# Softmax row sums of a 32-head attention: DMA chains that begin where ACT writes, all partial sums joined by DMA, one ones' product per head

## What is computed

```python
x = x + 0.5 * ffn(layernorm(x))             # weights are signs
x = x + attention(layernorm(x))
x = x + 0.5 * ffn(layernorm(x))

q, k, v = proj(w_q), proj(w_k), proj(w_v)   # 2 batches x 16 heads, head size 32
scores = jnp.einsum('bhqd,bhkd->bhqk', q, k) * SCALE
probs = jax.nn.softmax(scores, axis=-1)     # over 2048 keys
attn = jnp.einsum('bhqk,bhkd->bhqd', probs, v)
```

## Time and profile before

| | us |
|---|---|
| median of three runs (lowest, highest) | 2971.15 (2968.48, 2972.31) |
| profiled execution | 2973.73 |
| its span, first to last instruction | 2971.9 |
| PE busy | 2902.3 (98%) |
| DVE busy | 2038.9 (69%) |
| ACT busy | 1596.2 (54%) |
| POOL busy | 1382.4 (47%) |
| mean granted TensorE clock | 0.993 of full speed |

### The profile page before, as it was taken

The page is one execution under the profiler, slowest core; times in us unless marked ns, Lnnn a source line. Parts: engine busy times, 40 slices in busy tenths (PEclk is TensorE's granted clock), DMA queues, the critical chain, the costliest instruction groups (busy, mean ns, idle before and its releaser), DMA issues. The chain is left out here.

```text
span 2971.9 us, 38475 instructions
## 1 busy us (share of the span) xinstructions
PE 2902.3 (98%) x14528; PEld 1940.8 (65%) x14528; DVE 2038.9 (69%) x3036; ACT 1596.2 (54%) x2847; POOL 1382.4 (47%) x522
## 2 busy tenths in 40 slices
PE   7999998999999999999999999999999989999999
PEld 6888886887755555555555555555555458887887
DVE  5555555777788787878787888788888445555553
ACT  5444433332276666666666666666666644333333
POOL 0000000000089898988898988888888720000000
PEclk9999999999999999999999999999999999999999
DMA  4110112565398999898999898989898872222210
GB/s 184 30 56 29 29 34 79 185 197 169 123 224 199 226 202 231 200 234 198 228 204 229 202 232 201 228 203 231 203 228 208 212 209 57 57 57 57 57 29 29
DMA packets 189274, 459.97 MB, mean 155 GB/s; under 512 B 90272, under 2 KB 91296, under 8 KB 148768
## 3 DMA queue, kind: packets, MB, share of 16 engines
q0 software_dynamic: 36720, 267.40, 39.1%
q1 hardware_dynamic: 152368, 190.11, 22.4%
HBM read 121.91 MB, written 67.63 MB: 64 GB/s over the span
## 5 line engine op out<-in xcount | busy, mean ns | idle before, releaser
L918 DVE TENSOR_REDUCE att_row_max<-bank 128x1 f32<-128x512 f32 x2048 | 1255.3, 681 | 313.8 <-PE bank L989 313.7
L973 ACT ACTIVATE att_p<-bank 128x512 f32<-128x512 f32 x2048 | 1035.6, 629 | 411.9 <-PE bank L985 404.8
L874 POOL TENSOR_TENSOR att_acc<-att_acc,att_p 128x2048 f32<-128x2048 f32 x217 | 1063.4, 4901 | 34.3 <-ACT att_p L973 29.7
L985 PE MATMUL bank<-att_q,att_k 98*128 98x512 f32 x2048 | 849.6, 416 | 14.0 <-ACT att_p L973 9.2
L989 PE MATMUL bank<-att_k,att_q 96*128 96x512 f32 x2048 | 809.7, 397 | 11.0 <-DVE att_row_max L918 11.0
L985 PEld LDWEIGHTS bank<-att_q,att_k 98*128 98x128 f32 x2048 | 384.6, 188 | 391.4 <-issue 202.7
L1016 PE MATMUL bank<-att_p,att_v 128*32 128x512 f32 x4096 | 495.1, 600 | 0.0
L563 ACT ACTIVATE ffn_hid<-bank,up_s 128x512 f32<-128x512 f32 x256 | 176.1, 688 | 534.2 <-PE bank L591 519.8
L516 DVE TENSOR_TENSOR ffn_hid_lo<-ffn_hid,ffn_hid_hi 128x512 fp32r<-128x512 f32 x256 | 174.6, 687 | 376.5 <-ACT ffn_hid_hi L566 376.4
L989 PEld LDWEIGHTS bank<-att_k,att_q 96*128 96x128 f32 x2048 | 389.9, 190 | 61.7 <-DVE att_row_max L918 13.3
L591 PE MATMUL bank<-hi,ffn_up_w 128*128 128x512 f32 x1024 | 402.0, 393 | 3.8 <-DVE lo L189 3.8
(11 more groups left out here) (111 smaller groups left out, 2225.6 us busy)
## 6 DMA issues: line engine op xcount, KB each, us to landing
att_dma_acc<-att_p POOLq DMA_DIRECT2D x225, 1024.0 KB, 8.9
att_dma_acc<-att_dma_acc POOLq DMA_DIRECT2D x30, 1024.0 KB, 12.2
x<-x_after_ffn SPq DMA_DIRECT2D x16, 1024.0 KB, 7.5
att_q<-q_hi SPq DMA_DIRECT2D x64, 256.0 KB, 4.1
att_k<-k_hi SPq DMA_DIRECT2D x64, 256.0 KB, 10.1
x_after_ffn<-x_out SPq DMA_DIRECT2D x8, 1024.0 KB, 9.6
q_hi<-qkv_o_hi SPq DMA_DIRECT2D x32, 256.0 KB, 2.0
q_lo<-qkv_o_lo SPq DMA_DIRECT2D x32, 256.0 KB, 2.3
```

Source lines behind the costliest of these rows:

```text
L874: self.nc.gpsimd.tensor_tensor(self.acc[H % 2][:], a[:], self.prob[kt % PR][:], ALU.add).then_inc(self.summed, 1)
L918: self.nc.vector.tensor_reduce(self.row_max[odd][:, qt, q:q + 1], m[:], axis=AX.X, op=ALU.max).then_inc(self.m_read, 1)
L973: self.nc.scalar.activation(self.prob[kt % PR][:, q * CH:(q + 1) * CH], self.s_ps[(UNITS * H + kt * QC + q) % SR][:], ACT.Exp, scale=SCALE ...
L985: self.nc.tensor.matmul(self.s_ps[i % SR][:], self.k_st[H % NB][0:KM, kt * P:(kt + 1) * P], self.q_st[H % NB][0:KM, q * CH:(q + 1) * CH], ...
```

## The change

Three things change in how the denominators are made, and with them the places of four other steps.

1. `in_place(H, kt)` is true for the first tile of each chain (tiles 1 and 3). ACT writes these two directly into `dma_acc[H % 2][0]` and `[1]`, and PE's `out_tile` reads them there (`tile`). The two copying DMAs of a head are gone. The first adding DMA of each chain (tiles 5 and 7) now waits until PE has used that tile (`p_used`).
2. `join_sum` is a new adding DMA on POOL's queue, in the next head at tile 5: `acc` onto `dma_acc[..][0]`. It waits for POOL's last add, and for the landing of `join_chains`.
3. `sums` is one ones' product for heads 0 to 29 (`all_joined`) instead of two. It waits for the landing of `join_sum`, and stands after group 5 instead of 3. Heads 30 and 31 keep their three products.
4. Because the sums come later, ACT's `copy_sums` moves from tile 8 to tile 12 of the next head, SP sends `max_rows` before `move_sums`, and DVE's `invert` and SP's `store_inverse` come one head later (`invert` at tile 2).

The core of the diff:

```diff
-SUMS_AFTER = 3
+SUMS_AFTER = 5
 def sums_after(H):
-    return SUMS_AFTER if H < NH - 1 else SUMS_AFTER - 1
+    return SUMS_AFTER if H < NH - 1 else 2
-def chains_joined(H):
+def all_joined(H):
     return H < NH - 2
+def in_place(H, kt):
+    return kt in moved(H)[:CHAINS]
+    def tile(self, H, kt):
+        return self.dma_acc[H % 2][moved(H).index(kt)] if in_place(H, kt) else self.prob[kt % PR]
     def move(self, pool, H, kt):
+        if i // CHAINS == 1:
+            pool.wait_ge(self.p_used, KT * H + moved(H)[x] + 1)
-        if moved(H).index(kt) < CHAINS:
-            if H >= 2:
-                pool.wait_ge(self.t_ready, H - 1)
-            pool.sem_inc(self.move_begun, 1)
-            self.nc.gpsimd.dma_start(into[:], self.prob[kt % PR][:]).then_inc(self.dma_summed[x], 16)
+    def join_sum(self, pool, H):
+        pool.wait_ge(self.summed, all_adds(H))
+        pool.wait_ge(self.chains_joined, 16 * (H + 1))
+        if H > 0:
+            pool.wait_ge(self.sum_joined, 16 * H)
+        pool.sem_inc(self.move_begun, 1)
+        self.nc.gpsimd.dma_start(self.dma_acc[H % 2][0][:], self.acc[H % 2][:], accum_op=ALU.add).then_inc(self.sum_joined, 16)
-        if H > 0 and kt == (14 if H < NH - 1 else 12):
+        if H > 1 and kt == 2:
+            self.head_out.invert(dve, H - 2)
+        if H == NH - 1 and kt == 12:
             self.head_out.invert(dve, H - 1)
     def tile_free(self, act, H, kt):
+        if in_place(H, kt):
+            if H >= 2:
+                act.wait_ge(self.t_ready, H - 1)
+            return
     def sums(self, pe, H):
+        if all_joined(H):
+            pe.wait_ge(self.sum_joined, 16 * (H + 1))
+            self.ones_product(out, first, True, True).then_inc(self.t_ready, 1)
+            return
@@ SP, head H
                     if H > 0:
                         head_out.store_out(sp, H - 1)
+                    if H > 1:
+                        head_out.store_inverse(sp, H - 2)
+                    else:
+                        att.max_rows(sp, H + 1)
                     if H > 0:
                         head_out.move_sums(sp, H - 1)
-                    if H < LAST:
-                        att.max_rows(sp, H + 1)
@@ POOL, head H
                         if 0 < H < LAST and kt == 0:
                             att.join_chains(pool, H - 1)
+                        if 0 < H < LAST and kt == 5:
+                            att.join_sum(pool, H - 1)
```

More of the change, by code:

```diff
@@ L792, in moves_to @@
     i = moved(H).index(kt)
-    return sum(len(moved(h)[i % CHAINS::CHAINS]) for h in range(H)) + i // CHAINS + 1
+    return sum(len(moved(h)[i % CHAINS::CHAINS]) - 1 for h in range(H)) + i // CHAINS
 def all_adds(H):
@@ L903, in pool_tile @@
             self.add(pool, H, kt)
-        elif kt in moved(H):
+        elif kt in moved(H) and not in_place(H, kt):
             self.move(pool, H, kt)
@@ L967, in scalar_tile @@
         self.tile_free(act, H, kt)
+        into = self.tile(H, kt)
         if H > 0 and kt == G * (sums_after(H) + 1):
@@ L1015, in out_tile @@
             rows = slice(q * HD, (q + 1) * HD)
-            ins = self.nc.tensor.matmul(self.o_ps[rows, :], self.v_st[H % NB][:, kt, :], self.prob[kt % PR][:, q * CH:(q + 1) * CH],
+            ins = self.nc.tensor.matmul(self.o_ps[rows, :], self.v_st[H % NB][:, kt, :], self.tile(H, kt)[:, q * CH:(q + 1) * CH],
                                         start=(kt == 0), stop=(kt == KT - 1))
@@ L1027, in sums, with ones_product @@
     def sums(self, pe, H):
-        out, first, last = self.sums_bank(H), not direct(H), not chains_joined(H)
-        pe.wait_ge(self.summed, all_adds(H))
+        out, first = self.sums_bank(H), self.dma_acc[H % 2][0]
+        if all_joined(H):
+            pe.wait_ge(self.sum_joined, 16 * (H + 1))
+            self.ones_product(out, first, True, True).then_inc(self.t_ready, 1)
+            return
+        pe.wait_ge(self.summed, all_adds(H))
+        self.ones_product(out, self.acc[H % 2], not direct(H), False)
+        for x in range(CHAINS):
+            pe.wait_ge(self.dma_summed[x], 16 * all_moves(H, x))
+            ins = self.ones_product(out, self.dma_acc[H % 2][x], False, x == CHAINS - 1)
+        ins.then_inc(self.t_ready, 1)
+    def ones_product(self, out, tile, start, stop):
         for q in range(QC):
             rows = slice(q * HD, (q + 1) * HD)
-            self.nc.tensor.matmul(out[rows, :], self.ones_sum[:], self.acc[H % 2][:, q * CH:(q + 1) * CH], start=first, stop=False)
-        for x in range(CHAINS if last else 1):
-            if last:
-                pe.wait_ge(self.dma_summed[x], 16 * all_moves(H, x))
-            else:
-                pe.wait_ge(self.chains_joined, 16 * (H + 1))
-            for q in range(QC):
-                rows = slice(q * HD, (q + 1) * HD)
-                ins = self.nc.tensor.matmul(out[rows, :], self.ones_sum[:], self.dma_acc[H % 2][x][:, q * CH:(q + 1) * CH],
-                                            start=False, stop=(x == CHAINS - 1 or not last))
-        ins.then_inc(self.t_ready, 1)
+            ins = self.nc.tensor.matmul(out[rows, :], self.ones_sum[:], tile[:, q * CH:(q + 1) * CH], start=start, stop=stop)
+        return ins
     def bank_free(self, pe, H, at):
```

21 lines of the change are left out of this document (12 added, 9 removed).

## The result

Five runs beside five of the kernel before gave a median of 2955.86 us (2954.83 to 2960.73) against 2971.15 us (2968.48 to 2973.02): ratio 0.995, 95% interval 0.9937 to 0.9962. The change gains 15.3 us; the forecast was 2941, a gain of 30.2. The time lies just inside the upper edge of the range (2956), and the sum was twice too large.

The account below looks back on a forecast made before the run. PE's queue was taken to set the head. One ones' product fewer, head 31's end and head 1 summed to 25.8 + 4 + 1 = 30.8 us, from median 2971.15 to 2940.4, rounded to 2941; range 2934 to 2956.

Parts of the forecast that it names:

- What bounds the kernel: Ordinary heads: PE's queue, with work in 48.96 of 49.10 us, sets the head, with POOL close behind.
- rival A: POOL sets the head, which shortens by 3.7 us, 111 in 30 heads, giving 2860 us; chance 0.02.
- The product's price, 0.86: Heads 0 to 29: one ones' product fewer on PE saves 0.86 us each, 25.8 in all; its new place costs 0.
- rival B: Group 6 gets crowded or small waits return 12 to 20 us: 2950 to 2962 us; chance 0.14.
- The join of the accumulator: PE's new wait: the join lands at T = 29, 6 us before PE wants the sums; stall 0.
- Rival D: The accumulator's join lands after T = 35.4, PE waits 3.7 us a head: slower, 3056 us; chance 0.09.
- Tile 5's DMA: On POOL, behind the new wait: goes out at about T = 21.2 instead of 23.7; cost 0.
- SP's order: Maxima rows go no later; the sums behind them land 2.9 us before DVE wants them; cost 0, bounds 0 and 1 a head.
- So the queue carries 7 x 5.16 = 36.1 us a head after, 6 x 5.16 + 5.2 = 36.2 before: no more load: POOL's DMA queue with the copies gone: equal load, so no gain or cost in ordinary heads.
- Rival C: Next head's maxima rows come 0.9 us later in every head, so nothing is gained: about 2970 us; chance 0.06.
- The end of head 31: Without the two copies, POOL's load, scaling and last chain DMAs come earlier: gain 4 us, bounds 0 and 5.2.
- Head 1: POOL is late there from the extra split of output weights; an earlier POOL may give another 1 us, taken as 1.

Follow-up runs that it names:

- without_tile_9: Changed kernel without tile 9's adding DMA in heads 0 to 29, so it computes something else: 2939.00 us, ratio 0.9891.
- two_products: Changed kernel without the join of POOL's accumulator; PE makes two ones' products a head, after group 5: 2962.59 us, ratio 0.9967.
- turn_earlier_spread: Changed kernel, POOL's second feed-forward sign weights after DVE's, maxima six tiles ahead instead of four, early ones two a step at most: 2946.24 us.
- in_place_alone: Kernel before with only tiles 1 and 3 written in place by ACT and the two copies gone: 2964.33 us, ratio 0.9977.
- tile_13_behind_add: Changed kernel, POOL's second feed-forward sign weights after DVE's, tile 13's DMA issued behind POOL's add of tile 14: 3019.36 us.
- sums_sent_later: Changed kernel with SP's transfers of the sums, the reciprocal and its store one head later: 3062.14 us, ratio 1.0312.
- pool_after_dve: Changed kernel with POOL making its piece of the second feed-forward's sign weights only after DVE has made its own: 2949.99 us, ratio 0.9924.
- low_row_from_act: Changed kernel, POOL's second feed-forward sign weights after DVE's, second maxima row issued by ACT in tile 14 instead of SP: 2945.16 us.

## Why the prediction was right and wrong, step by step

- **What bounds the kernel: right.** Taking a product off PE's queue shortened the head wherever the rows were in time (48.02). The rule of the Trainium skill named in the prediction (Perfetto Trace Analysis, Identifying the Most-Contended Engine) would have made POOL the bound: the trace does not agree, POOL has as much work as before (1372.8 us, 1382.4 before), and the head followed PE (rival A).
- **The product's price, 0.86: right**, and its new place at no cost too (5.01 us for group 6, where over 4.3 + 0.86 would have been rival B). without_tile_9 gave 1.03 a head (49.05 - 48.02), two_products, which keeps both products, 0.11.
- **The join of the accumulator: right.** It was to land at T = 29 after 8.2 us; it landed at 27.2 after 7.9, and PE waited for it nowhere. Rival D, at 3056 the costly one, did not come.
- **Tile 5's DMA: right** (T = 21.2 forecast, 19.9 measured). **SP's order: right** as far as PE and DVE go: DVE does not wait for `head_tot_t`.
- **"So the queue carries 7 x 5.16 = 36.1 us a head after, 6 x 5.16 + 5.2 = 36.2 before: no more load", "No gain or cost in ordinary heads": the step that failed.** It put the price of the new order of POOL's transfers at nothing for the rows of the next head. The amount was right: q0's share of 16 engines was 39.1% of 2971.9 us before (1162 us) and is 38.4% of 2953.3 (1134). The conclusion was not. The copies stood early in the head, ahead of POOL's wait of 4.33 us, after which the queue ran in step; the new join stands 0.6 us ahead of tile 5's DMA and starts a backlog of one transfer that lasts to the turn. I had written that tile 5's transfer would land 5 us behind the join, and followed this only as far as tile 9. It should have been carried to tile 11, and from there to the rows. What the runs showed in its place: the rows land after 5.8 us instead of 4.2, PE waits for them, and a head takes 48.64 us where it takes 48.02 (without_tile_9) and 48.08 (turn_earlier_spread) when they are in time.
- **Rival C, given 0.06, came true** for about half of its price: of the 0.9 us that it named, the heads lost 0.45 against the forecast of 48.19 and 0.56 against 48.08. Its price of about 2970 (and D's 3056) left out the 4 + 1 us that the sum adds elsewhere; by the prediction's own terms C is 2966. "POOL is back in step with ACT when they are sent" was true of POOL's instructions and false of its DMA queue, which is another resource.
- **The end of head 31: wrong in both directions.** Bounds 0 and 5.2, taken 4, measured 12.2. The bound counted the queue time of the two copies alone; in_place_alone shows that their absence gives the 12 us by itself, with the waits of the earlier trace rows shortened one after the other. Which of these waits gave how much was not taken apart. And I did not ask what an earlier POOL would run into: DVE's work on the same weights, 5.5 us back.
- **Head 1: wrong**, +0.7 for -1.9. It took 52.3 in two_products and in_place_alone and 49.8 with the earlier turn. The reason isn't known.

**Partly open:** head 30 took 50.35 to 54.73 us in the profiled executions (67.5 in tile_13_behind_add, and 54.67 in sums_sent_later, both late for reasons of their own). In the other ten it goes with the granted clock. It stayed at the full level through head 30 in before, two_products and pool_after_dve, and the head took 50.35 to 51.37; in the seven others it was at the lower level for part of the head, which took 52.03 to 54.73. The changed kernel is one of these:

```profile
2305.00:2310.00 5.00, 5.00 (x27) 1.42 (x27) 0.91 (x2) 1.07 (x3) 5.00 (x3) 0.66 1.04 216
2310.00:2317.00 7.00, 6.55 (x25) 1.93 (x25) 0.56 (x2) 4.27 (x9) 7.00 (x4) 0.76 0.46 95
```

0.66 and 0.76 of full speed are mixtures of the two levels of 1.2 and 2.4 GHz. Each time PE had just waited 1.5 to 2.4 us for ACT's exponentials, or was still waiting (1.5 us at 2304.4 in the changed kernel). But it waited 1.5 to 1.7 us in the three with the full clock too, so what decides between them isn't known, and whether the 2.2 us of the changed kernel's head 30 belong to the change is open. SP's order wasn't tried by itself either, as sums_sent_later failed for another reason.

## What to carry to other kernels

Equal load on a DMA queue is not equal service: write out when each transfer is issued and when it lets the queue go, up to the moment at which a small, urgent transfer is sent beside it. An engine that is back in step says nothing of its DMA queue. And when an engine off the path becomes free earlier, look for the next instruction that it will start, and for who shares a port with it.

## What the runs showed of the hardware

- An 8 KB transfer on SP's queue took 1.8 us beside an emptying POOL queue and 5.8 us beside a full one (two_products, after), and landed there mostly 0.2 to 0.4 us behind the end of a 1 MB adding transfer. Issued from ACT's queue it took 5.5 (low_row_from_act).
- This has a limit. Sent a group earlier (turn_earlier_spread) the rows took 6.7 us, and 1 of 28 landed within 0.7 us behind the end of an adding transfer. There their first records started at most 5.0 us after the issue (median 4.7), in 18 of 28 heads in the midst of a transfer of POOL, 1.4 us or more behind the last 4-byte record that ended a share. For one head: the high row was issued at 1526.92, POOL's share ended at 1528.1 to 1528.2 on 15 engines without a record of the row, and the row's first records came at 1531.62 to 1531.92, between two 8 KB records. Why isn't known.
- DVE's 128 x 2048 `tensor_scalar` and `scalar_tensor_tensor` took 6.23 and 5.60 us beside POOL's, 1.16 and 2.29 alone.
- An adding DMA of 1 MB holds POOL's queue 4.9 to 5.3 us by the landings in the table above (6.1 once), and eight records of 0.63 us on each engine are 5.0.
